# Moving the value projections and the second half of x1, and issuing four attention units as two pairs, in a fused decoder layer

## The reference

```
x = x + attn(layernorm(x), Wq, Wk, Wv, Wo)    # 16 heads of 32 channels, causal over 512 tokens
x = x + xattn(layernorm(x), ctx, ctx)         # within each token: 16 heads of 16 channels attend to each other
x = x + ffn(layernorm(x))                     # x @ int4(kernel) + bias + (x @ a) @ b

attn:   q, k, v = x @ Wq, x @ Wk, x @ Wv      # (512, 512) per batch
        out = softmax(mask(q k^T / 4)) v, then out @ Wo
xattn:  scores[q, k] = sum_d x[q, d] ctx[k, d] / 4 for each token, causal over the 16 heads
        out[q, d] = sum_k softmax(scores)[q, k] ctx[k, d]
```

## Time and profile before

| | us |
|---|---|
| median of three runs | 817.64 |
| profiled execution, its own time | 820.83 |
| span of the profile | 818.9 |
| PE busy | 759.8 |
| DVE busy | 600.8 |
| POOL busy | 484.7 |
| ACT busy | 401.7 |
| mean granted TensorE clock | 0.985 of full speed |

### The profile page before, as it was taken

One profiled execution on the slowest core, in us unless ns is written; L12 is line 12 of the kernel. 1 busy time (PEld: TensorE's weight loads), 2 busy tenths in 40 slices (PEclk: granted clock), 3 DMA queues, 4 the chain that ended last, 5 costly groups with the idle time before them and its releaser, 6 DMA issues.

```text
span 818.9 us, 16251 instructions
## 1 busy us (share of the span) xinstructions
PE 759.8 (93%) x5757; PEld 535.3 (65%) x5757; DVE 600.8 (73%) x1227; ACT 401.7 (49%) x760; POOL 484.7 (59%) x452
## 2 busy tenths in 40 slices
PE   8788999989998999999999999998999898889998
PEld 6555565756675557666666666666766564488996
DVE  3544455456778886889788977887788878798774
ACT  5124555455645556546655573656465547551111
POOL 5000000032876889579968795879587879975442
PEclk9998999999999999999999999999999999997999
DMA  5886666866686668667856765677467750101001
GB/s 185 111 105 104 78 80 84 136 85 86 85 135 85 84 86 136 80 83 116 128 72 85 112 91 100 84 112 93 74 87 116 92 80 8 59 14 39 1 14 40
DMA packets 47982, 70.57 MB, mean 86 GB/s; under 512 B 4897, under 2 KB 22578, under 8 KB 47922
## 3 DMA queue, kind: packets, MB, share of 16 engines
q1 hardware_dynamic: 46898, 69.52, 56.8%
q10 hardware_dynamic: 1024, 0.26, 0.2%
HBM read 14.98 MB, written 4.19 MB: 23 GB/s over the span
## 4 chain that ended last, share of the span: by engine, by line
PE 65%; DVE 12%; DMA 10%; ACT 7%; issue 4%; SPq 1%; POOL 1%; ACTq 0%; DVEq 0%; POOLq 0%
PE misc L524 19%; PE exp_bank L524 17%; PE max_bank L524 10%; DMA stack_k<-k_lo 9%; PE acc_bank L524 9%; PE sum_bank L524 8%; DVE neg_max L1225 3%; DVE head_out L1237 3%; ACT probs L950 2%; ACT x_in L910 1%; PE misc L574 1%; ACT values L903 1%; SPq L455 1%; PE misc L641 1%; DVE x L1262 1%
## 5 line engine op out<-in xcount | busy, mean ns | idle before, releaser
L950 ACT ACTIVATE probs<-exp_bank 128x512 f32<-128x512 f32 x320 | 186.0, 594 | 202.4 <-PE sum_bank L524 109.8
L1225 DVE TENSOR_REDUCE neg_max<-max_bank 128x1 f32<-128x512 f32 (+1 forms) x192 | 130.3, 684 | 108.8 <-PE max_bank L524 107.6
L1602 POOL TENSOR_TENSOR prod<-head_probs,ctx_sb 128x256 f32<-128x256 f32 (+1 forms) x100 | 181.8, 1851 | 2.2 <-POOL head_probs L1597 0.5
L524 PE MATMUL max_bank<-stack_k,stack_q 96*128 96x384 f32 (+3 forms) x512 | 155.4, 365 | 13.9 <-DMA stack_k<-k_lo 7.7
L524 PE MATMUL exp_bank<-stack_q,stack_k 97*128 97x384 f32 (+3 forms) x512 | 149.8, 354 | 15.7 <-ACT probs L950 14.8
L314 POOL TENSOR_TENSOR prod<-x1n,ctx_sb 128x256 f32<-128x256 f32 (+1 forms) x104 | 158.2, 1554 | 4.6 <-ACT x1n L910 4.6
L1536 POOL TENSOR_TENSOR ln_var<-ln_mv,eps 128x4 f32<-128x4 f32 x21 | 4.4, 211 | 198.2 <-DVE ln_mv L1211 198.2
L524 PEld LDWEIGHTS exp_bank<-stack_q,stack_k 97*128 97x128 f32 x512 | 83.2, 192 | 48.4 <-ACT probs L950 23.4
L1225 DVE TENSOR_REDUCE seg_max<-max_bank 128x4 f32<-128x512 f32 x128 | 86.9, 685 | 37.8 <-PE max_bank L524 36.9
L524 PEld LDWEIGHTS max_bank<-stack_k,stack_q 96*128 96x128 f32 x512 | 86.0, 198 | 20.9 <-DMA stack_k<-k_lo 9.3
L524 PE MATMUL acc_bank<-probs,values 128*32 128x512 f32 (+3 forms) x1024 | 96.5, 447 | 0.9 <-ACT probs L950 0.9
(11 more groups left out here) (185 smaller groups left out, 1384.6 us busy)
## 6 DMA issues: line engine op xcount, KB each, us to landing
stack_q<-q_hi SPq DMA_DIRECT2D x64, 256.0 KB, 4.9
stack_k<-k_hi SPq DMA_DIRECT2D x64, 256.0 KB, 9.2
stack_q<-q_lo SPq DMA_DIRECT2D x32, 256.0 KB, 7.0
stack_k<-k_lo SPq DMA_DIRECT2D x32, 256.0 KB, 10.7
x_in<-in_x SPq DMA_DIRECT2D x9, 512.0 KB, 6.0
ctx_sb<-in_ctx SPq DMA_DIRECT2D x32, 128.0 KB, 3.1
x<-in_x SPq DMA_DIRECT2D x7, 512.0 KB, 10.2
out<-y_sb SPq DMA_DIRECT2D x5, 512.0 KB, 3.2
```

The source lines that it names most:

```text
L524: return nc.tensor.matmul(*args, **kw)
L950: nc.scalar.activation(probs[:, (UNITS * g + n) % PTR, :], exp_bank[n % 2][:, :], ACT.Exp, scale=SCALE).then_inc(exp_done, 1)
L1225: vec.tensor_reduce(o, v, axis=AX_X, op=ALU.max, negate=True).then_inc(max_taken, 1)
L1602: last = gp.tensor_tensor(pv_prod[:, COFF[j]:COFF[j + 1]].rearrange("p (q d k) -> p q d k", q=4, k=keys), head_probs[:, 4 * j:4 * j + 4, N ...
```

## The change

A new helper `values_due` says in which group and at which n a half of the values is projected and copied. All halves go through `misc[0]`. In g0 they are at n = 3 and 5. Those that belonged to g2 are at n = 3 of g2 (half 0) and at n = 5 of g3 (half 1). In g1, DVE's `add_to_x1(1)` comes directly after the maximum of unit 0, ahead of the value sums, and these are spread over n = 1 and n = 2. The calls of `attend` for four units become two calls for two units each.

```
+        def values_due(i, g, n):
+            at = {0: (0, {3: 0, 5: 1}), 2: (2, {3: 0}), 3: (2, {5: 1})}.get(g)
+            if not at or n not in at[1] or (i, at[0]) == FIRST_PASS:
+                return None
+            pair, half = values_pair(i, at[0]), at[1][n]
+            return (pair[1], half) if pair else None
...
             def project_v(pair, half):
-                bank = take(1 - half, v_ready, r_v)
+                bank = take(0, v_ready, r_v)
...
                             if n in (5, 9):
-                                attend(range(n - 5, n - 1), st["C"][1], first_tile)
+                                for pair in ((n - 5, n - 4), (n - 3, n - 2)):
+                                    attend(pair, st["C"][1], first_tile)
...
-                        if values_pair(i, g) and n in (0, 5) and (i, g) != FIRST_PASS:
-                            project_v(values_pair(i, g)[1], n // 5)
+                        if values_due(i, g, n):
+                            project_v(*values_due(i, g, n))
...
                 copy(values[:, 2 * pair:2 * pair + 2, 2 * half:2 * half + 2, :],
-                     misc[1 - half][:, :].rearrange("p (t s n) -> p s t n", t=2, s=2)).then_inc(v_ready, 1)
+                     misc[0][:, :].rearrange("p (t s n) -> p s t n", t=2, s=2)).then_inc(v_ready, 1)
...
-                        if values_pair(i, g) and n == 1 and (i, g) != FIRST_PASS:
-                            keep_values(values_pair(i, g)[1], 0)
...
-                        if values_pair(i, g) and n == 5 and (i, g) != FIRST_PASS:
-                            keep_values(values_pair(i, g)[1], 1)
+                        if values_due(i, g, n):
+                            keep_values(*values_due(i, g, n))
                         if g == 3 and ok(i + 2) and n in (5, 5 + 1):
                             layernorm(0, x_in, x_in, n - 5)
...
-                        if added and n == 0:
+                        late_sums = g == 1 and ok(i - 1)
+                        if late_sums and n == 1:
+                            add_to_x1(1)
+                        if added and n == (1 if late_sums else 0):
                             dve.wait_ge(hpv_prod, n_pv.up())
                             wait(dve, x2_ready, n_pv.now(1))
                             value_sums((3,))
...
-                        if g == 1 and ok(i - 1) and n == 1:
-                            add_to_x1(1)
                         if g == 1 and ok(i - 1) and n in (1, 2):
                             dve.wait_ge(x1_added, n_wo.now(2 - n))
                             ln_statistics(1, x1, n - 1)
-                        if added and n == 0:
+                        if added and n == (1 if late_sums else 0):
                             value_sums((2,))
-                        if added and n == 0:
+                        if added and n == (2 if late_sums else 0):
                             value_sums((0, 1)).then_inc(hpv_sum, 1)
```

## The result

The changed kernel takes 811.25 us (median of ten runs, 808.67 to 815.25) against 818.12 for the kernel before in the same sessions: ratio 0.9915, interval 0.9893 to 0.9937. It is 6.9 us faster. The forecast was 806 from 817.64, a gain of 11.6; the range (802 to 818) holds the result. The profiled execution took 815.25 (span 813.5), the slowest of the ten.

A forecast was written before the change was run, and what follows sets the result against it. PE's work plus its own waits was taken to bound the kernel. Passes summed 0.6 - 0.3 - 1.6 - 7.5 - 2.4 - 1.4 = -12.6 us, rounded down to 11.6 from 817.64: 806 us, range 802 to 818.

The forecast's parts named there:

- The wait at g0's n = 5: In g0, PE's 0.76 us wait for ACT's exponential of unit 3 would go, covered by the moved values.
- The -2.4: Change of g2 per pass: -2.8 us for values and waits, 0.4 given back because DVE begins late.
- limit of 18.4 us per group: Stack DMAs: 14.4 us from first issue to scoring plus 4.0 of other work; a shorter group waits.
- g3 pays for the values in full: Half 1 at n = 5 of g3 adds 1.5 us, as ACT cannot use the time; bounds 0 and +2.
- DVE in g1: Value sums after the maximum keep DVE busy longer, so PE waits until 0.8 us later each pass.
- the pairs pay for it: In g1 the exponential of unit 5 starts 0.75 us earlier, paying for DVE's 0.8; g1 in all 0.0.
- the boundary between pairs costs nothing: In attend, two pairs share one tiling mode, so none of the 64 boundaries costs PE time.
- the rival's +12 us: Attend's pair boundary costs 0.3 us, 64 times: +12 in the pairs-only run's expectation, +19 in the prediction; chance 0.10.
- The forecast's other estimate: At attend's 64 pair boundaries, each further semaphore increment adds about 26 ns: 1.7 us if all on the path.
- The rival of the limits: Stack DMAs and DVE in g1 each take 0.5 to 1 us of a pass: 811 to 812 us; chance 0.18.
- the last rival: More than forecast: values in g3 fill half of ACT's hole, -0.8 in each of six passes, 801 us; chance 0.08.
- a third of the third: Share counted as faster of the given-back case (g3's values and g1's pairs cost more, 814 to 818 us; chance 0.12).

The follow-up runs named there:

- e1: The kernel before with the values' move alone, without the x1 order or the pairs: 812.94 us, ratio 0.9923 to the kernel before.
- e2: The kernel before with only DVE's new x1 order in g1: 828.48 us, ratio 1.0118 to the kernel before.
- e10: The changed kernel with ACT's layernorm part ahead of the copy of the values in g3: 811.13 us, ratio 0.9923 to the kernel before.
- e3: The kernel before with only attend's four units as two pairs: 816.52 us, ratio 0.9984 to the kernel before.
- e9: The changed kernel with idle matmuls in PE's long waits in g1, g3, passes 0 to 2 and pass 7: 806.72 us, ratio 0.9864 to the kernel before.
- e5: The changed kernel with 16 idle matmuls ahead of PE's wait for DVE's maximum in g1, passes 2 to 6: 812.91 us, ratio 0.9946 to the kernel before.
- e4: The changed kernel with DVE's old order in g1: 814.75 us, ratio 0.9934 to the kernel before.
- e6: The changed kernel with value sums of chunks 3 and 2 at n = 0, chunks 1 and 0 at n = 1: 810.95 us, ratio 0.9906 to the kernel before.
- e7: The changed kernel with q projected at the end of n = 0, its high part copied before the maxima: 821.55 us, ratio 1.0031 to the kernel before.

## Why the prediction was right or wrong

**Right: the length of each group of the steady pass.** g0 by 0.2 us, g1 by 0.1, g2 exactly, g3 by 0.1. The values' move carries the gain: e1, without the two other parts, is not told apart from the changed kernel. The wait at g0's n = 5 is gone as forecast.

**Right by luck: g2.** The -2.4 was -2.8 for the moved values, less 0.4 because DVE would begin g2 late. The first term holds: pass 4's g2, where nothing waits, takes 19.61 us, 2.9 less than before. The second has the right size and the wrong cause. In passes 3 and 5 PE waits for the stack DMA. These are the rows of unit 0 of the later group in g2, for pass 3 (g2 starts at 347.32) and pass 4 (431.70):

```profile
348.93 0.49 PE L533 MATMUL max_bank<-stack_k,stack_q 96*128 96x512 f32 x1 [0.30 <-DMA stack_k<-k_lo]
```

```profile
432.81 0.48 PE L533 MATMUL max_bank<-stack_k,stack_q 96*128 96x512 f32 x1
```

This is 1.61 us into the group against 1.11, and the 0.5 us is what g2 takes longer. e2 has DVE's new order alone, and its g2 is 0.4 us shorter, not longer. The prediction had the numbers: unit 0 came 15.4 us after q_hi's issue, and without the values (1.54) and their late start (0.35) that is 13.5, less than the 14.2 to 14.4 that the DMAs take. Its limit of 18.4 us per group missed this, because it counts 4.0 us from a group's start to q_hi's issue, and in g1 it is 9.4 (from 431.82 - 21.90 = 409.92 to 419.31).

**Right: g3 pays for the values in full.** ACT's timeline in g3 of pass 4 of the changed kernel, units 5 and 6, has the order of the argument, and PE's wait for units 8 and 9 is still there (0.71 and 0.47 us of idle time):

```profile
460.98 0.58 ACT L960 ACTIVATE probs<-exp_bank 128x512 f32<-128x512 f32 x1
463.35 0.60 ACT L913 ACTIVATE values<-misc 128x512 f32<-128x512 f32 x1 [1.79 <-PE misc L533]
463.85 1.08 ACT L920 ACTIVATE x_in<-x_in,ln_bias,ln_rstd 128x256 f32<-128x256 f32 x2
464.83 0.58 ACT L960 ACTIVATE probs<-exp_bank 128x512 f32<-128x512 f32 x1
465.31 1.08 ACT L920 ACTIVATE x_in<-x_in,ln_bias,ln_rstd 128x256 f32<-128x256 f32 x2
```

e10 took this wait out and showed the DMA behind it.

**Right: DVE in g1, though not behind it.** The part costs g1 0.7 us alone (e2, forecast 0.8), PE's wait for the maximum rose from 0.40 to 1.4. That the pairs pay for it holds in sum (g1 21.82), and e3's g1 gives their share, 0.7. What neither term had is that g2 takes most of such a change back: 0.4 of e2's 0.7, and all of e3's 0.7.

**Right: the boundary between pairs costs nothing.** The attend takes 341.49 - 339.64 = 1.85 us as pairs; before it was 1.86 from its first matmul at 462.96 to 464.82 in g3. In e3 the rival's +12 us are not there. This agrees with the Trainium skill, "TensorEngine Tiling (Array Packing)", Key Properties, where a change of tile within one mode drains nothing. The forecast's other estimate, 1.7 us for the further increments, is below what these runs resolve (e3's interval spans 2.9 us).

**Wrong: the sum, in a term that it did not have.** The forecast priced a wait at its length: "waits until 0.8 us later" in g1, and in passes 0 and 1 "what the transposes gain (0.8 to 0.9) is all that can be had". The waits came about as forecast, but PE's clock fell after some of them. In pass 4 this cost the group 1.6 us and the pass 1.1, more than the 1.0 by which the wait itself had grown. Four of the six further falls are gone in e9: there pass 1 takes 82.01 us instead of 84.51, pass 4 82.71 instead of 83.87, pass 6 81.64 instead of 82.76, together 4.8 us, or 1.1 to 1.3 a fall. The profiled execution gained 5.6 us; with these four taken out it would have gained 10.4, where the sum had 12.6. What is still missing is in pass 0 (1.4 us above its forecast) and in the first three groups of pass 7 (1.9 above), where the two other falls are; how much of it is the clock isn't separated. I had read 0.985 as a clock that never mattered, though I had forecast myself that g1's wait would grow by 0.8 us, from that of the earlier trace rows.

The first guess at the place was wrong too. e5 cured g1 only and the time did not move: the clock now fell in g3. In e1, e4 and e5 the steady passes' falls sit in g3, in g2 and in g3. So it isn't tied to one wait. The falls return in every other pass in the changed kernel (422.1 and 589.3) though the wait is 1.3 to 1.4 us in each; what picks the pass, these runs don't show.

**The rival of the limits** had the measured number (811 to 812) for another reason. The limits are real: the changed kernel meets the stack DMA in g2 already, and e4, e6 and e10, which each remove another wait, meet it at once. But in the steady pass this costs nothing beyond the sum, where the 0.4 for DVE stood in for it.

**The chances** have an error of addition: the forecast, the limits, the last rival and a third of the third are 0.82, not 0.79.

**What stays open.** Pass 0's g0 took 25.4 us before and 26.0 after in the profiles, and between 23.8 and 27.0 in the experiments. Most of this goes with the clock: 23.8 with 3.4 us at the lower level in this group (e2, e3), 25.4 to 26.0 with 6.8 us (before, after and all others but e1), 27.0 with 10.2 (e1), 1.0 to 2.2 us for each 3.4. What sets the length of the stay is open, and so are the 0.6 us between before and after. Whether e4 is really slower than the changed kernel isn't either.

## What to carry to other kernels

Price a wait on TensorE by its length and by the clock behind it: where an edit lengthens a wait, ask whether the clock will fall, and compare the mean clock of the runs, not only the waits. Idle matmuls in waits that can't be removed were worth 4.5 us of 811 here between the medians (0.5% by the ratios), but only once most of the long waits had them; in one alone (e5) they showed nothing.

Where several limits stand one behind the other (here DVE's list, the stack DMAs and ACT's order), cures tried singly on the changed kernel show nothing, or even cost (1.003 for the early q alone), and together give 1.8% on it, 2.6% on the kernel before.

## What the runs showed of the hardware that was not expected

The same wait of 1.3 to 1.4 us was followed by the lower clock in passes 4 and 6 and not in 3 and 5 of one execution. Two waits for ACT of 0.7 and 0.5 us, whose ends are 1.5 us apart, were followed by it too (g3, in passes 3 to 5 of e1 and in pass 5 of e5). A stay at the lower clock took 3.4 us each time in the steady passes of the changed kernel and 6.8 in g1 of four passes of e7; one of 10.2 us came after 7.9 us without a gap. Ten runs of one kernel spread over 0.8% (808.67 to 815.25 us), and their mean clocks, 0.969 to 0.981, go with it.
